# Output projection of two tiles at once in rounded parts and rests, half of the features a step

## The reference

```
norm = adaln(x, cond)                   # block sums, keys, softmax over 8 blocks, layer norm
q, k, v = split(norm @ W_attn + b_attn) # 32 heads of 8 features
probs = softmax(mask(q k^T / sqrt(8)) + alibi)
x1 = x + (probs @ v) @ W_proj + b_proj  # the change is in this projection
h_t = GRU(h_{t-1}, x1_t)                # 32 steps, one after the other
out = x1 + h @ (W_ffn * scale)^T + b
```

## Time and profile before

| | |
|---|---|
| median of 3 runs | 487.22 us (486.86 to 487.56) |
| profiled execution | 486.86 us, of which the span 485.1 us |
| PE busy | 438.2 us (90%) |
| DVE busy | 343.6 us (71%) |
| ACT busy | 241.1 us (50%) |
| POOL busy | 108.4 us (22%) |
| mean granted TensorE clock | 0.972 |

### The profile page before, as it was taken

How to read it: one execution, slowest core, us unless ns; L and a number is a source line. 1 busy time by engine, 2 the same in 40 slices (tenths; PEclk the granted TensorE clock), 3 DMA queues, 4 the chain that set the end, 5 groups by cost and what they waited for, 6 DMA issues and landing times.

```text
span 485.1 us, 13494 instructions
## 1 busy us (share of the span) xinstructions
PE 438.2 (90%) x5458; PEld 359.0 (74%) x5458; DVE 343.6 (71%) x1015; ACT 241.1 (50%) x561; POOL 108.4 (22%) x119
## 2 busy tenths in 40 slices
PE   7679789899898998998989786999999999999995
PEld 5247467667676785776767675979998999899984
DVE  3815388789787987888888885366677767676665
ACT  1252545756648457466486454444444444444342
POOL 7330334443334445333251221000000000000000
PEclk9759899999999999999999999999999999999999
DMA  8511411332503314123130220000100001010101
GB/s 302 228 43 35 143 44 34 89 104 64 155 20 92 111 41 129 64 74 95 29 95 20 62 66 3 1 2 1 43 23 24 22 24 45 0 45 2 43 23 65
DMA packets 34268, 30.36 MB, mean 63 GB/s; under 512 B 4128, under 2 KB 29344, under 8 KB 34208
## 3 DMA queue, kind: packets, MB, share of 16 engines
q1 hardware_dynamic: 34208, 29.51, 19.1%
HBM read 16.91 MB, written 8.39 MB: 52 GB/s over the span
## 4 chain that ended last, share of the span: by engine, by line
PE 68%; DVE 14%; issue 7%; ACT 5%; SPq 3%; DMA 2%; POOL 1%; DVEq 0%; ACTq 0%; POOLq 0%
PE ps_a L1066 7%; PE ps_s L1271 6%; PE ps_t L1271 6%; PE ps_o L1271 6%; PE ps_s L1243 5%; PE ps_s L1115 5%; PE ps_t L1243 4%; PE ps_a L1075 4%; PE ps_a L1243 4%; PE ps_m L1243 3%; PE ps_m L1157 3%; PE ps_o L1139 3%; PE ps_t L1128 3%; SPq L332 2%; PE ps_a L1013 2%
## 5 line engine op out<-in xcount | busy, mean ns | idle before, releaser
L469 POOL TENSOR_TENSOR sc<-masked,mx 128x512 f32<-128x512 f32 x32 | 46.2, 1445 | 123.8 <-DVE mx L792 123.8
L1066 PE MATMUL ps_a<-yT_r,w_qkv_r 128*128 128x512 f32 x192 | 51.5, 418 | 1.5 <-ACT yT_r L527 1.5
L784 DVE COPY_PREDICATED masked<-kst,ps_s 128x512 f32<-128x512 int32 x64 | 44.0, 734 | 9.7 <-PE ps_s L1115 6.3
L1066 PEld LDWEIGHTS ps_a<-yT_r,w_qkv_r 128*128 128x128 f32 x192 | 36.5, 198 | 10.4 <-issue 2.1
L561 ACT ACTIVATE sc<-sc 128x512 f32<-128x512 f32 x64 | 37.1, 622 | 7.6 <-DVE sc L798 6.2
L792 DVE TENSOR_REDUCE mx<-masked 128x16 f32<-128x512 f32 x64 | 40.4, 672 | 0.0
L647 ACT ACTIVATE zg<-ps_t,brz 128x128 f32<-128x128 f32 x64 | 20.0, 364 | 38.8 <-PE ps_t L1271 38.8
L929 DVE SCALAR_TENSOR_TENSOR rg<-ps_o,vec,rg 128x128 f32<-128x128 f32 x64 | 19.5, 346 | 27.3 <-PE ps_o L1271 23.4
L1157 PE MATMUL ps_m<-oT,w_p 128*128 128x128 f32 x256 | 35.4, 282 | 3.6 <-ACT oT L491 3.6
L491 ACT ACTIVATE pT<-ps_t 128x512 f32<-128x512 f32 x64 | 35.0, 599 | 4.2 <-PE ps_t L1128 3.5
L1115 PE MATMUL ps_s<-kbd,qn 64*32 64x256 f32 x1024 | 35.9, 390 | 0.7 <-DMA kbd<-kn 0.7
(11 more groups left out here) (116 smaller groups left out, 872.8 us busy)
## 6 DMA issues: line engine op xcount, KB each, us to landing
xf<-in_x_feat SPq DMA_DIRECT2D x8, 512.0 KB, 4.2
xg<-in_x_tok SPq DMA_DIRECT2D x8, 512.0 KB, 5.0
kbd<-kn SPq DMA_DIRECT2D x128, 32.0 KB
v_dram<-vn SPq DMA_DIRECT2D x16, 256.0 KB, 2.5
vbd<-v_dram SPq DMA_DIRECT2D x64, 64.0 KB, 2.0
out_feat<-ost SPq DMA_DIRECT2D x16, 256.0 KB, 2.0
w_qkv<-in_wqkv SPq DMA_DIRECT2D x1, 768.0 KB, 7.5
w_ih<-in_wih SPq DMA_DIRECT2D x1, 768.0 KB, 10.2
```

Source lines behind the costliest of these rows:

```text
L469: nc.gpsimd.tensor_tensor(shifted, kept, m.unsqueeze(2).to_broadcast([P, NH // 2, S]), ALU.subtract).then_inc(sc_sub[1], 1)
L784: nc.vector.copy_predicated(kept, keep.unsqueeze(1).to_broadcast([P, NH // 2, S]), ps_s[:, h * 512:(h + 1) * 512].rearrange("p (h k) -> p ...
L1066: last = nc.tensor.matmul(bank, w_qkv_r[a][:, c, first_col + m * P:first_col + (m + 1) * P], yT_r[b][:, c, :], start=(a == b == c == 0), s ...
```

## The change

`oT` goes; the transposed output is copied by ACT into a rounded part `oT_r[0]` that holds two pairs of tiles, and a new DVE instruction a tile (`rest_of_attn`) computes the rest `oT_r[1]` from PSUM. The projection of a pair of tiles (256 columns) is done for one half of the output features in a step: steps j = 2 pair and 2 pair + 1 do m = 0 and m = 1. It works two steps behind (`project_out(n - 2)`) and it is moved, on PE, from before `cond_col` and `work_ahead` to directly before `probs_v`. `residual(j)` becomes one instruction over 8 batch rows and one half of the features. The weights get a rounded part (ACT, once) and a rest (DVE, once). Some buffers share space in another order.

```
 DVE   def rest_of_attn(n):
+          dve.wait_ge(ot_hi, n + 1)
+          nc.vector.tensor_tensor(attn_pair(1, n), ps_m[:, 0:E]..., attn_pair(0, n), ALU.subtract).then_inc(ot_lo, 1)
       def residual(j):
+          pair, m = j // 2, j % 2
+          dve.wait_ge(x1_mm, j + 1)
+          xs = xf[:, m, g, :, b0:b0 + 2 * TB].rearrange("p t b -> p b t")
+          nc.vector.scalar_tensor_tensor(xs, ps_m[:, E:2 * E]..., b_out[:, m:m + 1], xs, ALU.add, ALU.add)
-          for c in range(C):   # two instructions, one tile, both halves
 DVE   tile_step:
           softmax_mask(n + 1, ...)
+          if n > 0:
+              rest_of_attn(n - 1)
           cond_sums / cond_normalise / token_stats, softmax_max, softmax_shift, cond_scores
-          if n > 0:
-              residual(n - 1, ...)
+          if n > 1:
+              residual(n - 2)
           rest_of_proj
 PE    def project_out(j):
+          pair, m = j // 2, j % 2
+          pe.wait_ge(ot_lo, min(j + 2, NT))
+          pe.wait_ge(x1_out, j)              # j = 0: wp_lo
+          for a, b in ((0, 0), (1, 0), (0, 1)):
+              for c in range(C):
+                  last = nc.tensor.matmul(ps_m[:, E:2 * E], w_p_r[a][:, c, m * P:(m + 1) * P],
+                                          oT_r[b][:, pair % 2, c, :], ...)
 PE    tile_step:
           transpose_attn(n - 1), transpose_probs(n)
-          if n > 0:
-              project_out(n - 1)
           cond_col, work_ahead, cond_row, block_products, batch_proj
+          if n > 1:
+              project_out(n - 2)
           probs_v(n)
           spread_proj
 PE    end:
-          project_out(NT - 1)
+          for j in range(NT - 2, NT):
+              project_out(j)
 DVE   end:
-          residual(NT - 1, ...)
+          rest_of_attn(NT - 1)
+          residual(NT - 2)
+          residual(NT - 1)
 ACT   +   copy_out(w_p_r[0][:, :, :], w_p[:, :, :]).then_inc(wp_hi, 1)     # after the three w_qkv copies
 DVE   +   nc.vector.tensor_tensor(w_p_r[1], w_p, w_p_r[0], ALU.subtract)  # after rest_of_weights(2)
```

More of the change, by code:

```diff
@@ L96, in adaln_attn_gru_ffn @@
         on = sb("on", [P, E])
-        oT = sb("oT", [P, C, P])
         kw_sb = sb("kw_sb", [P, 2, E])
@@ L121, in adaln_attn_gru_ffn @@
         w_kwo = sb("w_kwo", [P, C, 2 * E])
-        w_p, w_f = (sb(n, [P, C, E]) for n in ("w_p", "w_f"))
+        w_f = sb("w_f", [P, C, E])
+        w_p_r = [sb(f"w_p_r{k}", [P, C, E], F32R) for k in range(2)]
         w_ih = sb("w_ih", [P, C, 3 * E])
@@ L133, in adaln_attn_gru_ffn @@
         w_qkv_r = [sb(f"w_qkv_r{k}", [P, C, 3 * E], F32R) for k in range(2)]
-        with ExitStack() as first_group_only:
-            w_qkv = first_group_only.enter_context(nc.sbuf_tensor("w_qkv", [P, C, 3 * E], F32))
+        with ExitStack() as until_last_norm:
+            w_qkv = until_last_norm.enter_context(nc.sbuf_tensor("w_qkv", [P, C, 3 * E], F32))
+            w_p = until_last_norm.enter_context(nc.sbuf_tensor("w_p", [P, C, E], F32))
+            xg = until_last_norm.enter_context(nc.sbuf_tensor("xg", [P, GT, E], F32))
+            y = until_last_norm.enter_context(nc.sbuf_tensor("y", [P, GT, E], F32))
         w_ih_r = [sb(f"w_ih_r{k}", [P, C, 3 * E], F32R) for k in range(2)]
@@ L147, in adaln_attn_gru_ffn @@
             pT = attention_only.enter_context(nc.sbuf_tensor("pT", [P, NQ, P], F32))
-            xg = attention_only.enter_context(nc.sbuf_tensor("xg", [P, GT, E], F32))
-            y = attention_only.enter_context(nc.sbuf_tensor("y", [P, GT, E], F32))
+            oT_r = [attention_only.enter_context(nc.sbuf_tensor(f"oT_r{k}", [P, 2, C, 2 * P], F32R)) for k in range(2)]
             yT = attention_only.enter_context(nc.sbuf_tensor("yT", [P, C, GC], F32))
@@ L246, in adaln_attn_gru_ffn @@
         ot_mm = sem("ot_mm")
-        ot_out = sem("ot_out")
+        ot_hi = sem("ot_hi")
+        ot_lo = sem("ot_lo")
+        wp_hi = sem("wp_hi")
+        wp_lo = sem("wp_lo")
         x1_mm = sem("x1_mm")
@@ L276, in adaln_attn_gru_ffn, with attn_pair @@
         proj_ps = ps_a[0:MH, 0:E]
+        zeros = oT_r[0][:, 0, 0, :].bitcast(F32)
+        def attn_pair(k, n):
+            return oT_r[k][:, n // 2 % 2, :, n % 2 * P:(n % 2 + 1) * P]
         def x_group(g):
@@ L413, in _ @@
         def _(pool):
-            nc.gpsimd.memset(oT[:, :, :], 0.0).then_inc(warm_zeros, 1)
+            nc.gpsimd.memset(zeros, 0.0).then_inc(warm_zeros, 1)
             nc.gpsimd.memset(minus_half[:, :], -0.5).then_inc(pool_consts, 1)
@@ L571, in attn_out @@
                 act.wait_ge(ot_mm, n + 1)
-                copy_out(oT[:, :, :].rearrange("p c n -> p (c n)"), ps_m[:, 0:E]).then_inc(ot_out, 1)
+                if n % 2 == 0 and n >= 4:
+                    act.wait_ge(x1_mm, n - 2)
+                copy_out(attn_pair(0, n), ps_m[:, 0:E].rearrange("p (c n) -> p c n", c=C)).then_inc(ot_hi, 1)
             cond_out(0, ps_a[:, 0:512], first=True)
@@ L582, in _ @@
                 copy_out(w_qkv_r[0][:, :, cols], w_qkv[:, :, cols]).then_inc(wqkv_hi, 1)
+            copy_out(w_p_r[0][:, :, :], w_p[:, :, :]).then_inc(wp_hi, 1)
             cond_out(1, ps_m[:, :])
@@ L630, in tile_step @@
                         act.wait_ge(wqkv_lo, 3)
+                        act.wait_ge(wp_lo, 1)
+                        act.wait_ge(bv_mm, 1)
                         act.wait_ge(w_ready, 2)
@@ L665, in round_input @@
                              ).then_inc(x_hi, 1)
-            act.wait_ge(x1_out, C * (B // TB))
+            act.wait_ge(x1_out, B // TB)
             for u in range(3):
@@ L812, in normalise, with rest_of_attn, residual @@
                     ALU.mult).then_inc(o_norm, 1)
-            def residual(n, g, i):
-                dve.wait_ge(x1_mm, n + 1)
-                for c in range(C):
[L820 to L823, removed]
+            def rest_of_attn(n):
+                dve.wait_ge(ot_hi, n + 1)
+                nc.vector.tensor_tensor(attn_pair(1, n), ps_m[:, 0:E].rearrange("p (c n) -> p c n", c=C),
+                                        attn_pair(0, n), ALU.subtract).then_inc(ot_lo, 1)
+            def residual(j):
+                pair, m = j // 2, j % 2
+                g, b0 = pair // GH, pair % GH * 2 * TB
+                dve.wait_ge(x1_mm, j + 1)
+                xs = xf[:, m, g, :, b0:b0 + 2 * TB].rearrange("p t b -> p b t")
+                nc.vector.scalar_tensor_tensor(
+                    xs, ps_m[:, E:2 * E].rearrange("p (b t) -> p b t", b=2 * TB),
+                    b_out[:, m:m + 1], xs, ALU.add, ALU.add).then_inc(x1_out, 1)
             dve.wait_ge(wq_done, 1)
@@ L842, in _ @@
             rest_of_weights(2)
+            dve.wait_ge(wp_hi, 1)
+            nc.vector.tensor_tensor(w_p_r[1][:, :, :], w_p[:, :, :], w_p_r[0][:, :, :], ALU.subtract).then_inc(wp_lo, 1)
             dve.wait_ge(filled, 2)
@@ L909, in tile_step @@
                     rest_of_gru_weights(i - 1)
-                if n > 0:
-                    residual(n - 1, (n - 1) // GT, (n - 1) % GT)
+                if n > 1:
+                    residual(n - 2)
                 if norm_ahead and i == 1:
@@ L918, in _ @@
             normalise(NT - 1)
-            residual(NT - 1, NG - 1, GT - 1)
+            rest_of_attn(NT - 1)
+            residual(NT - 2)
+            residual(NT - 1)
             def state(t):
@@ L989, in emit_last @@
                         emit_step(f, m, 2 * half + e, bank[:, (2 * m + e) * B:(2 * m + e + 1) * B])
-            dve.wait_ge(x1_out, C * (B // TB))
+            dve.wait_ge(x1_out, B // TB)
             for u in range(3):
@@ L1150, in transpose_attn, with project_out @@
                 last.then_inc(ot_mm, 1)
-            def project_out(n):
-                pe.wait_ge(ot_out, n + 1)
-                for m in range(C):
+            def project_out(j):
+                pair, m = j // 2, j % 2
+                pe.wait_ge(ot_lo, min(j + 2, NT))
+                if j == 0:
+                    pe.wait_ge(wp_lo, 1)
+                else:
+                    pe.wait_ge(x1_out, j)
+                for a, b in ((0, 0), (1, 0), (0, 1)):
                     for c in range(C):
-                        last = nc.tensor.matmul(ps_m[:, E + m * P:E + (m + 1) * P], w_p[:, c, m * P:(m + 1) * P],
-                                                oT[:, c, :], start=(c == 0), stop=(c == C - 1))
+                        last = nc.tensor.matmul(ps_m[:, E:2 * E], w_p_r[a][:, c, m * P:(m + 1) * P],
+                                                oT_r[b][:, pair % 2, c, :], start=(a == b == c == 0),
+                                                stop=(b == 1 and c == C - 1))
                 last.then_inc(x1_mm, 1)
@@ L1163, in keep_warm @@
                 for _ in range(products):
-                    nc.tensor.matmul(ps_t[:, 0:256], oT[:, 0, :], oT[:, :, :].rearrange("p c n -> p (c n)"),
-                                     start=True, stop=True)
+                    nc.tensor.matmul(ps_t[:, 0:256], zeros[:, 0:P], zeros, start=True, stop=True)
```

(2 more changed lines are left out.)

## The result

The changed kernel takes 506.31 us (503.67 to 509.72, 4 runs) where the kernel before takes 487.04 (485.13 to 487.56, 4 runs): a ratio of 1.0404, 95% interval 1.0366 to 1.0441. The sign was forecast, the size was not: +19 us measured, +10 forecast, outside the range given. The profiled execution took 505.84 us with a span of 503.9, 18.8 more than the span before.

A forecast was written before the change was run, and what follows sets the result against it. PE (29.24 of some 31.5 us a group) bounds only in parts; steps 0 and 1 wait for DVE. Terms 0.4 - 0.7 + 9.4 - 0.9 + 0.3 + 1.6 = +10.1 us gave 497.3 on the median, range 490.5 to 501.5.

The forecast's parts named there:

- The rival that PE bounds throughout: Whole kernel: new projection and DVE additions find cover, PE sheds 6 us, less the tail's 1.6: -4.4, 482.8; chance 0.13.
- Step 0: Groups 1 to 5: new projection between `cond_row` and `probs_v` is on the chain, +0.70 a group, bound +1.3.
- Step 1: Groups 1 to 5: `cond_col` 0.37 later, `rest_of_proj` 0.90 later behind projection and residual, +1.27 a group, bounds 1.1 and 1.4.
- Steps 2 and 3: Groups 1 to 5: PE loses 0.19 and DVE gains 0.20 in each; -0.1 for both, bounds -0.4 and +0.4.
- 0.70 us is on the chain: Step 0: price of the new projection behind the `cond_row` wait, 6 products at 0.1175 us each.
- The cover of the rest by L443: Step 0: second sum L701 still ends with POOL's L443, so DVE's rest costs nothing there; other bound 0.6.
- Group 5: Attention stage: priced like the other groups of 1 to 5, +1.87.
- The end: Group 6 -0.9 (projection leaves the k products' front), group 7 +0.3, tail +1.6; GRU stage untouched.
- The rival of the falling clock: Step 0 of each group: longer PE waits lower the clock, some 1.4 us each, +7, 504; chance 0.05.
- The rest of the weights: Prologue: DVE's rest of the weights (0.64) delays POOL's operations before the first normalisation, +0.4, bounds 0 and 0.6.
- Group 0: Step 1: old projection (0.89) removed with no new one yet, limited by DVE 0.37 later: -0.7.
- The rival at its top: Sums not covered by L443, +0.6 in step 0 of five groups, steps 2 and 3 at upper bound: 501.5; chance 0.08.

The follow-up runs named there:

- The run with the other order on DVE: The changed kernel with `rest_of_proj` ahead of the residual on DVE in step 1; 503.67 us, ratio 1.0351 to the kernel before.

## Why the prediction was right or wrong

**The mechanism was right, the sum too small.** The forecast put the loss where it is: the projection behind `cond_row` and behind `batch_proj`, the residual ahead of `rest_of_proj`, PE's shed work worth nothing. The rival that PE bounds throughout is refuted from two sides: the old product in the new place costs as much a group as the whole change, and without the rest, in PE's waits, the new product only draws level.

**Which steps failed.** The profiled span grew by 8.7 more than the sum said. The largest part, 4.9, is the granted clock at the end: the sum had it at nothing, and it stood only in a rival of 0.05. Groups 1 to 4 took 3.3 more, half of it the price of the projection on the chain; group 5 alone took 1.4 more. The start and the rest of the end came out within 0.5 of the forecast. The clock alone didn't make the miss: the changed kernel's fastest execution, with the highest mean clock of its four (0.976), took 503.67, which is above the range too.

**Steps 0 and 1 of groups 1 to 5: the terms that were mis-sized.** Step 0, from the opening transposes to DVE's `normalise` (153.96 to 163.30 before, 158.72 to 169.24 after), went from 9.34 to 10.52: +1.18 where 0.70 was forecast. Step 1, from there to the end of `spread_proj` (at 172.39 before, 179.85 after), from 9.09 to 10.61: +1.52 where 1.27 was. Steps 2 and 3 gave back nothing where 0.10 was forecast. The term that was mis-sized is the projection at "0.70 us is on the chain": it took 0.90 and 0.92 there. The price was read from 24 products in an unbroken row; behind a long run of products it is 0.70 also in the changed kernel (184.95 in the chain above). In steps 0 and 1 it stands behind one short fp32 product (two matmul records). There the loading of its first weights starts only 0.07 ahead of its piece of the chain (at 167.49 and 176.84), in step 2 it starts 0.28 ahead (184.67) and in step 3, where the price is 0.71, 0.59 ahead (189.87). The later start goes with the higher price; that it is the cause was not tested. In the tail the prediction had added "0.2 of drain and start", and had not in the steps. The old product shows the same: 1.10 in the new place, 0.89 in the old. The rest of the gap is smaller: the residual of step 1 counts with 0.69 and not 0.61, the sums of step 0 put `cond_row` 0.16 later, and `cond_row` and `probs_v` themselves count 0.12 more in step 0. The forecast also rounded 0.70 + 0.61 - 0.44 up to 0.90.

**The cover of the rest by L443 held, though in another form.** The forecast had L701 still end with L443. Now the first sum (L714) is the one that is held, 0.98 in place of 0.4, and the second runs behind it in 0.34. Of the 0.6 that the rest could have cost, 0.16 came through. Both sums have two inputs in SBUF, the rest has one in PSUM and wasn't held. The Trainium skill's rule (SBUF — State Buffer, "Who interferes with whom") names this class; the trace agrees: L714 took 0.98 while POOL's L453 ran, and L832, in the same stretch with one input in PSUM, its usual 0.42. What the prediction drew from it, that only L701 meets the cover, was its own slip.

**Group 5** lost 3.3 (28.97 to 32.25). It has no block products in step 3, so the projection there waits 0.59 for DVE's rest; the forecast had priced it as the others.

**The end.** Forecast +1.0 for groups 6, 7 and the tail and nothing for the GRU stage; measured +3.4 and +2.0. Where the clock stayed up, 4.9 of this 5.4 went, so the arithmetic of the forecast there was about right (+0.5 in place of +1.0, in the profiles of two kernels) and the clock was left out of it. The tail alone, from the last transposes of the attention output to the first input product, went from 4.37 before to 6.25 in the run with the other order on DVE: +1.9 where 1.6 was forecast. The rival of the falling clock had a chance of 0.05 and was placed in step 0 of every group. In the profiled execution it came true in the last two groups and the tail only; in other executions it came in single groups, at 1.5 a time in two of them.

**The start.** The rest of the weights was forecast at +0.4. POOL's first of three operations took 0.62 before and 1.99 in the changed kernel's profile, 1.99 again in one later profile with the same rest, 0.62 in four others, and 1.39 in that of the old product in the new place, which has no such rest. The opening of group 0 came at 57.06 before, at 57.76 in the changed kernel and between 56.87 and 57.98 in the other five, so 0.4 is inside what changes from run to run. Group 0 gave back 1.3 in the profile where 0.7 was forecast, but the clock is part of that: in its first 8 us it was 0.50 and 0.66 before and 1.00 after. The run with the other order on DVE, with 0.57 and 0.58 there, has a group 0 of 32.71 against 33.35 before, 0.64 less, as forecast.

**The range** reached to 501.5. The rival at its top was added up short: 0.6 and 0.5 more in each of five groups are 5.5 and not 4 to 5. Besides, it had bounds for each term alone; what it lacked is that the largest unknowns (the price of a product outside a long run, the clock in longer waits) all go the same way once PE waits more.

What stays open: what makes PE stand still between score products in some executions (0.51, 0.88 and 2.24 us in three of the profiles), and how much of the changed kernel's spread of 6 us is this and how much the clock.

## What to carry to other kernels

Work of the engine with the highest busy share is free as long as it stands ahead of a wait for another engine, and has its full price behind it: ask of a moved product first which wait it fills, and only then what it costs. Whatever then waits for its result on another in-order engine, here the residual ahead of `rest_of_proj`, is moved onto the chain with it. A product outside a long run can cost more than its share of one, here 0.9 in place of 0.7. And where the clock falls in some executions only, one profile of each kernel says what a fall costs, but not what a filler does against it: for that, look at the mean clock of every execution.

## What the runs showed of the hardware

The same products cost the chain more behind a short one: 6 products of 256 columns took 0.90 to 0.92 behind one short fp32 product and 0.70 behind a long run, the 8 fp32 records 1.10 and 0.89. The granted clock fell to 1.2 GHz in one group of each of two profiles after two waits of 1.40 and 1.52 with 4.3 us between them, and in the other groups, with the same waits, did not; it fell at the end of one profile after waits of 1.38, 0.92, 0.93 and 0.83, and stayed up in another after waits of 1.37, 0.92, 0.93 and 0.83. The kernel before, with waits of 0.56 and 0.29 in the groups, spread over 2.4 us in its first four executions and the changed one over 6.0. A POOL operation of 0.20 took 0.62, 1.39 or 1.99 beside two or three DVE subtractions with both inputs in SBUF, ending 0.1 to 0.2 after the first, the second or the third of them.
